# Counting in a threshold search: VectorE masks folded by TensorE in place of counts by VectorE and ScalarE

## The chip, the core and the metric

One NeuronCore of a Trainium2 chip runs the whole kernel. Its engines run side by side and wait for each other through semaphores: TensorE (PE, with its weight loads as PEld), VectorE (DVE), ScalarE (ACT), GpSimd (POOL) and SyncE (SP), which issues DMAs. The metric is device time in microseconds, the median of several executions. The kernel before takes 1645.15 us (three runs, 1643.38 to 1646.12).

## The reference

The reference is a vision tower on 64 images: a patch embedding, one attention block, and a routed feed-forward block. The change lies in the last one, which in short is

```python
acts   = gelu(x @ input_patterns.T).mean(axis=1)          # per image: 2048 numbers
top, i = top_k(acts, 256)                                  # keep the 256 largest of 2048
p      = gelu(scatter(top, i) @ process_input_weights.T)   # per image: 1024 numbers
top, i = top_k(p, 128)
v      = softmax(top) @ process_values[i]                  # per image: 128 numbers
o      = gelu(v @ output_input_weights.T)                  # per image: 2048 numbers
top, i = top_k(o, 256)                                     # keep the 256 largest of 2048
out    = h + (top @ output_patterns[i])                    # the same row for every token
```

The two choices of 256 from 2048 are what is touched.

## The kernel before, in words

`tower` computes everything up to `acts` and stores `h`; `route` does the rest. In `route` the 2048 numbers of an image lie on two partitions of 1024 each (`wide`, 128 partitions x 1024): image b on partitions b and b + 64.

`wide_top_k` finds the 256th largest number of each image exactly. It turns the floats into sortable 32-bit keys and splits each key into two 16-bit words. A search (`look_through`) goes over the high words, a second one over the low words of the numbers that tie there. `wide_top_k` runs twice (`acts` and `o`), so there are four searches. A search has 8 rounds (`ROUNDS`), 32 in all. A round (`try_three`) settles two bits: it asks for three thresholds how many of the image's 2048 words reach each, counts on how many thresholds 256 are reached (`found`), and moves the lower bound by that many steps. `tried` holds the bound and the thresholds of the next round, and `ahead` is the part of the next `tried` that doesn't depend on the answer. The rounds are a strict chain: a round begins when `tried` of the round before is written.

In a round of the kernel before, three engines count:

- VectorE (L1252) compares all 1024 words with the first threshold and 640 of them (`SHARED_AT`) with the second, and adds up by the accumulator of the instruction (`accum_out`).
- ScalarE (`count_too`, L1173 and L1175) takes the Sign of the words against the third threshold, and of the other 384 words against the second; its sums of signs also come from an accumulator.
- TensorE (`sum_halves`, L1068 to L1072) adds the partial counts of the two partitions of an image, and turns signs into counts, by three matmuls of 4 columns with 128x128 matrices (`image_sum`, `image_minus_half`). The result is in one of two PSUM banks (`tallies`).

VectorE then compares three numbers with 256 (`passed`, L1258, with `found` as accumulator) and writes the next `tried` (L1263).

TensorE and ScalarE have other work in the first 16 rounds: `turn_table` transposes the 8 MB of `process_input_weights`, two tables of four 128x128 transposes behind each `sum_halves`, and ScalarE copies each table out of PSUM (`copy_table`, L1181). Each engine takes its instructions in program order, so the transposes of a round sit between two `sum_halves`. SP loads the next 1 MB of the weights when `turned` tells that a buffer is free. In the last 16 rounds neither engine has other work.

Of the kernel before, what the change touches and what calls it, by code (L numbers as in the profile page):

```python
# [20 lines left out]
F32R = mybir.dt.float32r  # L21
I32 = mybir.dt.int32
I16 = mybir.dt.int16
BF16 = mybir.dt.bfloat16
ALU = mybir.AluOpType
ACT = mybir.ActivationFunctionType
AX = mybir.AxisListType

P = 128
# [843 lines left out]
def route(nc, s, w, process_w, process_v, output_w, output_p, search_steps, h2_dram, out):  # L873
# [5 lines left out]
    with ExitStack() as ctx:  # L879
        def sb(name, shape, dt=F32):  # L880
            return ctx.enter_context(nc.sbuf_tensor(name, shape, dt))

        def sem(name):
            return ctx.enter_context(nc.semaphore(name))
# [4 lines left out]
        HALF = s.n_in // 2  # L889
        HALF_T = IN_T // 2  # L890
        ROUNDS = KEY_ROUNDS
        STAGE = 2 * ROUNDS
# [16 lines left out]
        word = sb("word", [P, HALF], I16)  # L909
        low_word = sb("low_word", [P, HALF], I16)  # L910

        reached = [chosen_t[:].bitcast(BF16)[:, n * HALF:(n + 1) * HALF] for n in range(2)]
        SHARED_AT = 5 * HALF // 8
        reached_too = sb("reached_too", [P, 2 * HALF - SHARED_AT], BF16)


        TOKENS = s.tokens // 2
# [27 lines left out]

        tried = sb("tried", [P, 5])
        ahead = sb("ahead", [P, 5])
        blank = sb("blank", [P, 12])
        numbers = sb("numbers", [P, 12], F32R)
        count, signs, offset = (numbers[:, n:n + 4] for n in (0, 4, 8))  # L950
        image_sum = sb("image_sum", [P, P], F32R)
        image_minus_half = sb("image_minus_half", [P, P], F32R)
        passed = sb("passed", [P, 3])
        found = sb("found", [P, 1])
        quota = sb("quota", [P, 1])
# [2 lines left out]

        turn = [ctx.enter_context(nc.psum_tensor(f"rt{b}", [P, 512], F32)) for b in range(3)]
        sums = ctx.enter_context(nc.psum_tensor("sums", [P, 512], F32))  # L960
        tallies = [sums, turn[2]]
        prod = [ctx.enter_context(nc.psum_tensor(f"rp{b}", [P, 512], F32)) for b in range(4)]

        process_in = [sem(f"process_in{n}") for n in range(2)]
        small_in, steps_in, masks_made, turned, copied = sem("small_in"), sem("steps_in"), sem("masks_made"), sem("turned"), sem("copied")
        acts_turned, wide_made, chosen = sem("acts_turned"), sem("wide_made"), sem("chosen")
        words_made, tried_made, numbers_made, counted, counted_too = sem("words_made"), sem("tried_made"), sem("numbers_made"), sem("counted"), sem("counted_too")
        summed, ahead_made, judged = sem("summed"), sem("ahead_made"), sem("judged")
        tie_step, ties_counted, ties_placed = sem("tie_step"), sem("ties_counted"), sem("ties_placed")
        taken, softmax = sem("taken"), sem("softmax")  # L970
# [52 lines left out]
        @block.gpsimd  # L1023
        def _(pool):

            pool.memset(other_half[:], 0.0).then_inc(masks_made, 1)
            pool.wait_ge(masks_made, 1)
            pool.affine_select(out=other_half[:], in_=other_half[:], compare_op=ALU.not_equal, fill=1.0, base=B,
                               pattern=[[-1, P]], channel_multiplier=1).then_inc(masks_made, 1)
            pool.wait_ge(masks_made, 2)  # L1030
            pool.tensor_tensor(same_image[:], other_half[:], w.ident[:], ALU.add).then_inc(masks_made, 1)
            pool.wait_ge(masks_made, 3)
            pool.affine_select(out=same_image[:], in_=same_image[:], compare_op=ALU.not_equal, fill=1.0, base=-B,
                               pattern=[[-1, P]], channel_multiplier=1).then_inc(masks_made, 1)
            pool.memset(blank[:], 0.0).then_inc(masks_made, 1)
            pool.wait_ge(masks_made, 5)
            pool.memset(blank[:, 9:10], (HALF - SHARED_AT) / 2)
            pool.memset(blank[:, 10:11], HALF / 2).then_inc(masks_made, 1)
            pool.memset(values[:, :, s.d_pv:], 1.0).then_inc(masks_made, 1)

        @block.tensor
        def _(pe):

            for t in range(HALF_T):
                last = pe.transpose(turn[t // 4][:, (t % 4) * P:(t % 4 + 1) * P], w.acts[:, t * P:(t + 1) * P],
                                    w.ident[:])
                if t % 4 == 3:
                    last.then_inc(acts_turned, 1)
            pe.wait_ge(masks_made, 7)

            def turn_table(f):
                r, first = tables[f]
# [7 lines left out]

            def sum_halves(n):

                tally = tallies[n % 2][:, 0:4]
                if n == 0:
                    pe.wait_ge(numbers_made, 1)
                if n >= 2:
                    pe.wait_ge(judged, n - 1)
                pe.matmul(tally, image_sum[:], offset, start=True, stop=False)  # L1068
                pe.wait_ge(counted_too, n + 1)
                pe.matmul(tally, image_minus_half[:], signs, start=False, stop=False)  # L1070
                pe.wait_ge(counted, n + 1)
                pe.matmul(tally, image_sum[:], count, start=False, stop=True).then_inc(summed, 1)  # L1072

            def place_ties(stage):

# [84 lines left out]
        def _(act):  # L1160
# [2 lines left out]
                last = act.activation(wide[:, n * 512:(n + 1) * 512], turn[n][:], ACT.Copy, scale=1.0 / s.tokens)  # L1163
            last.then_inc(wide_made, 1)

            def count_too(n, search):


                act.wait_ge(tried_made, n + search + 1)
                if n == 0:  # L1170
                    act.wait_ge(numbers_made, 1)
                with nc.allow_low_precision(reason="whole numbers up to 1024"):
                    act.activation(reached_too[:, 0:HALF], word[:], ACT.Sign, scale=-1.0, bias=tried[:, 4:5],  # L1173
                                   accum_out=signs[:, 2:3])
                    act.activation(reached_too[:, HALF:], word[:, SHARED_AT:], ACT.Sign, scale=-1.0,  # L1175
                                   bias=tried[:, 3:4], accum_out=signs[:, 1:2]).then_inc(counted_too, 1)

            def copy_table(f):
                r, first = tables[f]
                act.wait_ge(turned, f + 1)  # L1180
                act.activation(process_t[:, first:first + 4, r * P:(r + 1) * P],  # L1181
                               prod[f % 4][:].rearrange("p (e j) -> p e j", e=4), ACT.Copy).then_inc(copied, 1)


            act.wait_ge(masks_made, 7)
            act.activation(image_sum[:], same_image[:], ACT.Copy)
            act.activation(image_minus_half[:], same_image[:], ACT.Copy, scale=-0.5)
            act.activation(numbers[:], blank[:], ACT.Copy).then_inc(numbers_made, 1)
            act.activation(both_halves[:], same_image[:, 0:B].unsqueeze(2).to_broadcast([P, B, 2]), ACT.Copy)
            for n in range(STAGE):  # L1190
                count_too(n, n // ROUNDS)
                if n >= 1:
                    copy_table(2 * n - 2)
                    copy_table(2 * n - 1)
            copy_table(fills - 2)
            copy_table(fills - 1)

            def keep_chosen(banks, done):
                for n in range(banks):
# [21 lines left out]
                act.wait_ge(output_product, n + 1)  # L1221
                last = act.activation(wide[:, n * 512:(n + 1) * 512], prod[n][:], ACT.Gelu)
            last.then_inc(wide_made, 1)
            for search in (2, 3):
                for n in range(ROUNDS):
                    count_too(search * ROUNDS + n, search)
            keep_chosen(2, 4)
            act.wait_ge(product, 3)
            act.activation(routed[0][:], prod[2][:, 0:D], ACT.Copy).then_inc(result, 2)
# [2 lines left out]
        def _(dve):  # L1232
# [8 lines left out]
            def look_through(search):  # L1241

                dve.tensor_scalar(tried[:], steps[:, 0:5], float(LOWEST), None, ALU.add).then_inc(tried_made, 1)
                dve.wait_ge(tried_made, search * (ROUNDS + 1) + 1)

                def try_three(search, r):
                    n, at = search * ROUNDS + r, 6 * r
                    if n == 0:
                        dve.wait_ge(numbers_made, 1)
                    with nc.allow_low_precision(reason="whole numbers up to 1024"):  # L1250
                        for m, cols in enumerate((HALF, SHARED_AT)):
                            last = dve.tensor_scalar(reached[m][:, 0:cols], word[:, 0:cols], tried[:, 1 + m:2 + m],  # L1252
                                                     0.0, ALU.is_ge, ALU.add, accum_out=count[:, m:m + 1])
                        last.then_inc(counted, 1)
                    dve.tensor_scalar(ahead[:], steps[:, at + 6:at + 11], tried[:, 0:1], None,
                                      ALU.add).then_inc(ahead_made, 1)
                    dve.wait_ge(summed, n + 1)
                    dve.tensor_scalar(passed[:], tallies[n % 2][:, 0:3], float(s.k_in), 0.0, ALU.is_ge, ALU.add,  # L1258
                                      accum_out=found[:]).then_inc(judged, 1)
                    dve.wait_ge(ahead_made, n + 1)  # L1260
                    dve.wait_ge(judged, n + 1)

                    dve.scalar_tensor_tensor(tried[:], found[:].to_broadcast([P, 5]), steps[:, at + 5:at + 6],  # L1263
                                             ahead[:], ALU.mult, ALU.add).then_inc(tried_made, 1)
                    dve.wait_ge(tried_made, n + search + 2)

                for r in range(ROUNDS):
                    try_three(search, r)
# [113 lines left out]
def search_steps():  # L1382

    size = 4.0 ** np.arange(KEY_ROUNDS - 1, -1, -1)
    rounds = np.stack([0 * size, size, 2 * size, 2 * size - 0.5, 3 * size - 0.5, size], axis=1)
    return np.tile(np.append(rounds.reshape(-1), np.zeros(6)), (P, 1)).astype(np.float32)


# [23 lines left out]
```

## Time and profile before

| | us |
|---|---|
| median of the runs | 1645.15 |
| the profiled execution's own time | 1649.54 |
| its span, from the first instruction to the last | 1647.8 |
| `tower`, to the last copy of `acts` | about 1414 |
| first search, first to last round | 1419.83 to 1444.55 |
| second search | 1447.53 to 1472.22 |
| third search | 1544.55 to 1569.25 |
| fourth search | 1572.23 to 1596.92 |

A timeline row gives the start in us from the span's start, the duration in us, the engine, the line of the code, the operation, what is written and read, the shape and the count; in brackets the idle time of the engine before it and what ended it. The clock column of the stretches (PEclk) is the TensorE clock that was granted, as a share of 2.4 GHz; 0.50 is 1.2 GHz.

### The profile page before, as it was taken

To read this page: it belongs to the slowest core of one execution; us is meant where nothing else is said; L and a number is where in the kernel's file an instruction comes from. 1 tells how busy PE (TensorE), PEld (TensorE's weight loads), DVE (VectorE), ACT (ScalarE), POOL (GpSimd) and SP (SyncE) were. 2 spreads that over 40 slices of the span, in tenths; PEclk is the share of its full clock that TensorE was granted. 3 is DMA by queue.
4 is the path that set the end of the run, shared out by engine and by line. 5 is a ranking of instruction groups with operands and counts; after the bars stand their busy time and mean duration, and the time that the engine had idled before them with its cause. 6 is when DMAs were issued, how large, how long until landed. Compare 5 with 4: busy or idle time off the path is not lost. (4 is left out here: it accounts for less than half of the span.)

```text
span 1647.8 us, 33024 instructions
## 1 busy us (share of the span) xinstructions
PE 1474.3 (89%) x10453; PEld 1420.8 (86%) x10453; DVE 1015.9 (62%) x2493; ACT 882.6 (54%) x3156; POOL 112.4 (7%) x243
## 2 busy tenths in 40 slices
PE   5899999999999999999999999999999998764321
PEld 4799999999999999999999999999999998761220
DVE  6766666656665666665665566566565643585686
ACT  3455555555555555555555555555555554761440
POOL 0000000000000000000000000000000000000000
PEclk9999999999999999999999999999999999757555
DMA  8211111111111111111111111111110000376007
GB/s 202 79 45 45 44 43 43 43 39 40 41 43 43 43 43 43 43 43 43 43 40 40 39 40 39 39 39 40 39 43 10 10 11 11 110 248 249 0 0 313
DMA packets 53094, 99.38 MB, mean 60 GB/s; under 512 B 16704, under 2 KB 35648, under 8 KB 52032
## 3 DMA queue, kind: packets, MB, share of 16 engines
q1 hardware_dynamic: 50768, 96.91, 19.0%
q10 hardware_dynamic: 2288, 2.00, 0.6%
q8 instruction: 19, 0.31, 0.1%
q14 instruction: 19, 0.16, 0.0%
HBM read 73.17 MB, written 25.69 MB: 60 GB/s over the span
## 5 line engine op out<-in xcount | busy, mean ns | idle before, releaser
L620 ACT ACTIVATE ffn<-ffn 128x196 f32<-128x196 f32 x1024 | 329.8, 322 | 220.8 <-PE ffn L511 220.2
L511 PE MATMUL ffn<-x_t_hi,pat_w_hi 128*128 128x392 f32 x1024 | 361.2, 353 | 1.7 <-DVE x_t_lo L783 1.7
L511 PE MATMUL ffn<-x_t_hi,pat_w_lo 128*128 128x392 f32 x1024 | 348.5, 340 | 0.0
L511 PE MATMUL ffn<-x_t_lo,pat_w_hi 128*128 128x392 f32 x1024 | 348.2, 340 | 0.0
L440 PE MATMUL gen<-qkvu_w_hi,h_t_hi 128*98 128x256 f32 x768 | 215.5, 281 | 1.2 <-ACT q_t L578 1.2
L440 PE MATMUL gen<-qkvu_w_hi,h_t_lo 128*98 128x256 f32 x768 | 215.0, 280 | 0.0
L440 PE MATMUL gen<-qkvu_w_lo,h_t_hi 128*98 128x256 f32 x768 | 214.9, 280 | 0.0
L511 PEld LDWEIGHTS ffn<-x_t_hi,pat_w_hi 128*128 128x128 f32 x1024 | 192.8, 188 | 4.1 <-DVE x_t_lo L783 2.0
L620 ACT ACTIVATION_READ_ACCUMULATOR ffn<-ffn 128x1 f32 x1024 | 194.1, 190 | 0.0
L511 PEld LDWEIGHTS ffn<-x_t_lo,pat_w_hi 128*128 128x128 f32 x1024 | 194.0, 189 | 0.0
L511 PEld LDWEIGHTS ffn<-x_t_hi,pat_w_lo 128*128 128x128 f32 x1024 | 192.7, 188 | 0.0
L719 DVE SCALAR_TENSOR_TENSOR shared<-shared,gen 98x512 f32<-98x512 f32 x64 | 44.0, 687 | 167.1 <-ACT shared L593 167.1
L679 DVE TENSOR_TENSOR patch_lo<-pixels,patch_hi 128x392 fp32r<-128x392 f32 x192 | 106.5, 559 | 58.8 <-ACT patch_hi L555 58.6
L394 PE MATMUL gen<-patch_hi,tok_w_hi 128*128 128x392 f32 x384 | 134.2, 350 | 1.6 <-DVE patch_lo L679 1.6
L394 PE MATMUL gen<-patch_hi,tok_w_lo 128*128 128x392 f32 x384 | 131.8, 343 | 0.0
L394 PE MATMUL gen<-patch_lo,tok_w_hi 128*128 128x392 f32 x384 | 131.0, 341 | 0.0
L440 PEld LDWEIGHTS gen<-qkvu_w_hi,h_t_hi 128*98 128x98 f32 x768 | 125.2, 163 | 1.7 <-ACT q_t L578 1.4
L440 PEld LDWEIGHTS gen<-qkvu_w_lo,h_t_hi 128*98 128x98 f32 x768 | 125.3, 163 | 1.5
L440 PEld LDWEIGHTS gen<-qkvu_w_hi,h_t_lo 128*98 128x98 f32 x768 | 125.3, 163 | 0.0
L673 DVE STREAM_TRANSPOSE pixels<-raw 128x448 f32<-128x448 f32 x192 | 111.7, 621 | 12.7 <-DMA raw<-in_x_dram 11.8
L562 ACT ACTIVATE h_t_hi<-gen,bias 128x392 fp32r<-128x392 f32 x64 | 37.6, 588 | 144.2 <-PE gen L394 141.0
L847 POOL TENSOR_SCALAR rstd<-moments 98x4 f32<-98x4 f32 x64 | 22.3, 349 | 1259.5 <-DVE moments L691 1181.0
(209 smaller groups left out, 2735.8 us busy)
## 6 DMA issues: line engine op xcount, KB each, us to landing
raw<-in_x_dram SPq DMA_DIRECT2D x752, 56.0 KB, 2.0
h_dram<-h SPq DMA_DIRECT2D x128, 98.0 KB
process_nat<-ocess_input_weights_dram SPq DMA_DIRECT2D x8, 1024.0 KB, 4.8
process_t<-h_dram SPq DMA_DIRECT2D x8, 896.0 KB, 11.7
out_dram<-process_t SPq DMA_DIRECT2D x8, 896.0 KB, 6.7
h_early<-h_dram SPq DMA_DIRECT2D x4, 896.0 KB, 12.1
out_dram<-h_early SPq DMA_DIRECT2D x4, 896.0 KB, 4.0
pat_nat<-_ffn_input_patterns_dram SPq DMA_DIRECT2D x1, 2048.0 KB, 16.0
```

What stands on the lines that cost most here:

```text
L394: last = pe.matmul(gb[TOK[m]][:, 0:T2], a[:, ks, m * P:(m + 1) * P], b[:, ks], start=n == 0, stop=n == 3 * s.ksubs - 1)
L440: last = pe.matmul(gb[bank][0:T, t * D:(t + 1) * D], a[:, d, tok_cols(img, t)], b[:, d, at:at + D], start=n == 0, stop=n == 3 * s.halves - 1)
L511: last = pe.matmul(fb[f % FFN_BANKS][:, 0:T2], a[:, d, f * P:(f + 1) * P], b[:, d, :], start=n == 0, stop=n == 3 * s.halves - 1)
L562: act.activation(h_ts[0][:, m], gb[TOK[m]][:, 0:T2], ACT.Identity, bias=w.bias[:, m:m + 1])
L620: last = act.activation(cols, cols, ACT.Gelu, accum_out=gelu_sum[:, par, at:at + 1])
L673: last = dve.transpose(pixels[:, 2 * c + h], raw[:, slot, h].rearrange("p i w j -> p w i j"))
L679: dve.tensor_tensor(patch_part(patch[1], ks), turned_pixels(ks), view(patch_part(patch[0], ks)), ALU.subtract).then_inc(patch_low, 1)
L719: dve.scalar_tensor_tensor(flat(gate[:, img]), flat(gate[:, img]), 1.0, gb[(0, 3)[img]][0:T, :], ALU.add, ALU.mult).then_inc(gate_made, 1)
L847: pool.tensor_scalar(rstd[:, which], moments[:, which, :, 1], LN_EPS, None, ALU.add).then_inc(pool_step, 1)
```

## The change

ScalarE no longer counts, and VectorE no longer uses the accumulator. VectorE writes, for each of the three thresholds, a mask of 1024 bf16 ones and zeros per partition (`reached[m]`; the first two lie in `chosen_t` as before, the third in a buffer of its own). For each mask TensorE runs 16 matmuls of 64 columns (`BLOCK`) with the same 128x128 matrix `image_sum`, now bf16, all into the same 64 columns of PSUM: this adds the two partitions of an image and folds 1024 columns into 64. TensorE waits for each mask by itself (`masked`). VectorE then sums the 3 x 64 numbers by a `reduce_sum` from PSUM (`counts`), waits for it, and goes on as before. One PSUM bank (`turn[2]`) takes the place of two. The third threshold is now a whole step, not a half step less as Sign needs it. The small constants for the signs go.

```diff
-        SHARED_AT = 5 * HALF // 8
-        reached_too = sb("reached_too", [P, 2 * HALF - SHARED_AT], BF16)
+        reached.append(sb("reached_last", [P, HALF], BF16)[:])
+        THRESHOLDS, BLOCK = len(reached), 64
...
-        image_sum = sb("image_sum", [P, P], F32R)
-        image_minus_half = sb("image_minus_half", [P, P], F32R)
+        image_sum = sb("image_sum", [P, P], BF16)
+        counts = sb("counts", [P, THRESHOLDS])
...
             def sum_halves(n):
-                tally = tallies[n % 2][:, 0:4]
                 if n == 0:
-                    pe.wait_ge(numbers_made, 1)
-                if n >= 2:
-                    pe.wait_ge(judged, n - 1)
-                pe.matmul(tally, image_sum[:], offset, start=True, stop=False)
-                pe.wait_ge(counted_too, n + 1)
-                pe.matmul(tally, image_minus_half[:], signs, start=False, stop=False)
-                pe.wait_ge(counted, n + 1)
-                pe.matmul(tally, image_sum[:], count, start=False, stop=True).then_inc(summed, 1)
+                    pe.wait_ge(image_sum_made, 1)
+                for m in range(THRESHOLDS):
+                    pe.wait_ge(masked, THRESHOLDS * n + m + 1)
+                    for at in range(0, HALF, BLOCK):
+                        last = pe.matmul(tally[:, m * BLOCK:(m + 1) * BLOCK], image_sum[:],
+                                         reached[m][:, at:at + BLOCK], start=at == 0, stop=at == HALF - BLOCK)
+                last.then_inc(summed, 1)
...
-            for n in range(STAGE):
-                count_too(n, n // ROUNDS)
-                if n >= 1:
-                    copy_table(2 * n - 2)
-                    copy_table(2 * n - 1)
-            copy_table(fills - 2)
-            copy_table(fills - 1)
+            for f in range(fills):
+                copy_table(f)
...
-            for search in (2, 3):
-                for n in range(ROUNDS):
-                    count_too(search * ROUNDS + n, search)
...
                 def try_three(search, r):
                     n, at = search * ROUNDS + r, 6 * r
-                    if n == 0:
-                        dve.wait_ge(numbers_made, 1)
-                    with nc.allow_low_precision(reason="whole numbers up to 1024"):
-                        for m, cols in enumerate((HALF, SHARED_AT)):
-                            last = dve.tensor_scalar(reached[m][:, 0:cols], word[:, 0:cols], tried[:, 1 + m:2 + m],
-                                                     0.0, ALU.is_ge, ALU.add, accum_out=count[:, m:m + 1])
-                        last.then_inc(counted, 1)
+                    for m in range(THRESHOLDS):
+                        dve.tensor_scalar(reached[m], word[:], tried[:, 1 + m:2 + m], None,
+                                          ALU.is_ge).then_inc(masked, 1)
                     dve.tensor_scalar(ahead[:], steps[:, at + 6:at + 11], tried[:, 0:1], None,
                                       ALU.add).then_inc(ahead_made, 1)
                     dve.wait_ge(summed, n + 1)
-                    dve.tensor_scalar(passed[:], tallies[n % 2][:, 0:3], float(s.k_in), 0.0, ALU.is_ge, ALU.add,
+                    dve.reduce_sum(counts[:], tally[:, 0:THRESHOLDS * BLOCK].rearrange("p (m b) -> p m b", b=BLOCK),
+                                   axis=AX.X).then_inc(counted, 1)
+                    dve.wait_ge(counted, n + 1)
+                    dve.tensor_scalar(passed[:], counts[:], float(s.k_in), 0.0, ALU.is_ge, ALU.add,
                                       accum_out=found[:]).then_inc(judged, 1)
...
-    rounds = np.stack([0 * size, size, 2 * size, 2 * size - 0.5, 3 * size - 0.5, size], axis=1)
+    rounds = np.stack([0 * size, size, 2 * size, 3 * size, 3 * size - 0.5, size], axis=1)
```

## Rows read from the trace of the kernel before

**Rows 1.** The page's chain that ended last, shares of the span by line.

```profile
ACT reached_too L1173 2%; PE rp L1097 1%; ACT reached_too L1175 1%; DVE process_t L1352 1%; DVE left L1323 1%; DVE ranked L1322 1%; DVE tried L1263 0%; PE sums L1070 0%; PE rt L1070 0%; DVE h_early L1352 0%; DVE chosen_t L1278 0%; DVE passed L1258 0%; PE rt L1085 0%; PE rp L1148 0%; PE rt L1072 0%
```

**Rows 2.** Timeline of one round of the third search.

```profile
1547.64 1.28 DVE L1252 TENSOR_SCALAR_CACHE_REDUCE chosen_t<-word,tried 128x1024 bf16<-128x1024 int16 x1
...
1548.84 0.88 DVE L1252 TENSOR_SCALAR_CACHE_REDUCE chosen_t<-word,tried 128x640 bf16<-128x640 int16 x1
...
1549.53 0.37 PE L1070 MATMUL rt<-numbers,image_minus_half 128*128 128x4 f32 x1 [2.25 <-ACT reached_too L1175]
1549.64 0.08 DVE L1252 DVE_READ_ACCUMULATOR chosen_t<-word,tried 128x1 fp32r x1
...
1549.78 0.37 PE L1072 MATMUL rt<-numbers,image_sum 128*128 128x4 f32 x1
1549.95 0.33 PEld L1068 LDWEIGHTS sums<-numbers,image_sum 128*128 128x128 f32 x1
...
1550.19 0.16 DVE L1258 TENSOR_SCALAR_CACHE_REDUCE passed<-rt 128x3 f32<-128x3 f32 x1 [0.32 <-PE rt L1072]
...
1550.47 0.23 DVE L1263 SCALAR_TENSOR_TENSOR tried<-found,steps,ahead 128x5 f32<-128x5 f32 x1
...
1550.73 1.28 DVE L1252 TENSOR_SCALAR_CACHE_REDUCE chosen_t<-word,tried 128x1024 bf16<-128x1024 int16 x1
```

**Rows 3.** Stretches (searches 1, 4): length; PE, PEld, DVE, ACT, POOL (count); clock; DMA.

```profile
1419.80:1444.50 24.70, 18.35 (x82) 17.75 (x83) 20.99 (x64) 21.47 (x46) 0.00 (x0) 0.50 0.42 157
...
1572.00:1597.00 25.00, 6.48 (x23) 5.79 (x23) 21.25 (x66) 14.71 (x32) 0.00 (x0) 0.50 0.00 0
```

**Rows 4.** Groups of VectorE by line and shape: busy us, mean ns, idle before.

```profile
L1252 DVE TENSOR_SCALAR_CACHE_REDUCE chosen_t<-word,tried 128x1024 bf16<-128x1024 int16 x32 | 40.9, 1279 | 1.1
...
L1255 DVE TENSOR_SCALAR ahead<-steps,tried 128x5 f32<-128x5 f32 x32 | 7.3, 227 | 0.0
...
L1299 DVE TENSOR_SCALAR sure<-word,tried 128x1024 f32<-128x1024 int16 x2 | 1.5, 754 | 0.1
...
L1334 DVE TENSOR_REDUCE kth<-least 128x1 f32<-128x129 f32 x1 | 0.3, 286 | 0.0
```

**Rows 5.** Groups of PE weight loads: same stationary operand twice, both loaded.

```profile
L497 PEld LDWEIGHTS gen<-wo_w_lo,g_t_hi 128*98 128x98 f32 x256 | 42.8, 167 | 0.0
...
L497 PEld LDWEIGHTS gen<-wo_w_hi,g_t_hi 128*98 128x98 f32 x256 | 42.6, 167 | 13.8 <-DVE g_t_lo L783 13.8
```

**Rows 6.** Timeline: 392-column matmuls at the granted clock 0.50, two in sequence.

```profile
1381.28 0.53 PE L511 MATMUL ffn<-x_t_hi,pat_w_lo 128*128 128x392 f32 x1
1381.60 0.53 PE L511 MATMUL ffn<-x_t_hi,pat_w_hi 128*128 128x392 f32 x1
```

**Rows 7.** Timeline: the same at the full clock, and 32 matmuls of 64 columns.

```profile
1324.91 1.01 PEld L455 LDWEIGHTS gen<-shared 98*64 98x64 f32 x32 [0.26 <-issue]
...
1326.46 0.34 PE L511 MATMUL ffn<-x_t_hi,pat_w_lo 128*128 128x392 f32 x1
...
1326.64 0.34 PE L511 MATMUL ffn<-x_t_hi,pat_w_hi 128*128 128x392 f32 x1
```

**Rows 8.** The same 64-column loads over the whole span, mean ns.

```profile
L455 PEld LDWEIGHTS gen<-shared 98*64 98x64 f32 x1024 | 32.5, 138 | 8.2 <-issue 8.2
```

**Rows 9.** Stretches with PE busy (first figure after the length) and granted clock.

```profile
1426.00:1429.10 3.10, 2.46 (x13) 2.38 (x13) 2.63 (x8) 2.81 (x6) 0.00 (x0) 0.50 0.25 45
1480.00:1482.00 2.00, 2.00 (x10) 1.62 (x11) 0.31 (x1) 0.83 (x2) 0.00 (x0) 0.50 1.01 419
...
1486.00:1488.00 2.00, 2.00 (x13) 0.56 (x9) 0.00 (x0) 0.00 (x0) 0.00 (x0) 1.00 1.01 419
1531.60:1535.40 3.80, 3.67 (x16) 3.30 (x16) 0.03 (x1) 0.00 (x0) 0.00 (x0) 0.50 0.00 0
...
40.00:42.00 2.00, 0.82 (x7) 0.58 (x6) 2.00 (x6) 2.00 (x6) 0.00 (x0) 1.00 0.41 118
```

**Rows 10.** Timeline of a round of the first search: the transposes behind the count.

```profile
1428.40 1.97 PE L1057 MATMUL rp<-ident,process_nat 128*128 128x128 f32 x8
```

More of the change, by code:

```diff
@@ L947, in route @@
         ahead = sb("ahead", [P, 5])
-        blank = sb("blank", [P, 12])
-        numbers = sb("numbers", [P, 12], F32R)
-        count, signs, offset = (numbers[:, n:n + 4] for n in (0, 4, 8))
-        image_sum = sb("image_sum", [P, P], F32R)
-        image_minus_half = sb("image_minus_half", [P, P], F32R)
+        image_sum = sb("image_sum", [P, P], BF16)
+        counts = sb("counts", [P, THRESHOLDS])
         passed = sb("passed", [P, 3])
@@ L960, in route @@
         sums = ctx.enter_context(nc.psum_tensor("sums", [P, 512], F32))
-        tallies = [sums, turn[2]]
+        tally = turn[2]
         prod = [ctx.enter_context(nc.psum_tensor(f"rp{b}", [P, 512], F32)) for b in range(4)]
@@ L966, in route @@
         acts_turned, wide_made, chosen = sem("acts_turned"), sem("wide_made"), sem("chosen")
-        words_made, tried_made, numbers_made, counted, counted_too = sem("words_made"), sem("tried_made"), sem("numbers_made"), sem("counted"), sem("counted_too")
+        words_made, tried_made, image_sum_made, counted, masked = sem("words_made"), sem("tried_made"), sem("image_sum_made"), sem("counted"), sem("masked")
         summed, ahead_made, judged = sem("summed"), sem("ahead_made"), sem("judged")
@@ L1034, in _ @@
                                pattern=[[-1, P]], channel_multiplier=1).then_inc(masks_made, 1)
[L1035 to L1038, printed above, removed]
             pool.memset(values[:, :, s.d_pv:], 1.0).then_inc(masks_made, 1)
@@ L1048, in _ @@
                     last.then_inc(acts_turned, 1)
-            pe.wait_ge(masks_made, 7)
+            pe.wait_ge(masks_made, 5)
             def turn_table(f):
@@ L1164, in _ @@
             last.then_inc(wide_made, 1)
-            def count_too(n, search):
-                act.wait_ge(tried_made, n + search + 1)
-                if n == 0:
-                    act.wait_ge(numbers_made, 1)
-                with nc.allow_low_precision(reason="whole numbers up to 1024"):
[L1173 to L1176, printed above, removed]
             def copy_table(f):
@@ L1182, in copy_table @@
                                prod[f % 4][:].rearrange("p (e j) -> p e j", e=4), ACT.Copy).then_inc(copied, 1)
[L1185 to L1188, printed above, removed]
+            act.wait_ge(masks_made, 5)
+            act.activation(image_sum[:], same_image[:], ACT.Copy).then_inc(image_sum_made, 1)
             act.activation(both_halves[:], same_image[:, 0:B].unsqueeze(2).to_broadcast([P, B, 2]), ACT.Copy)
-            for n in range(STAGE):
-                count_too(n, n // ROUNDS)
-                if n >= 1:
-                    copy_table(2 * n - 2)
-                    copy_table(2 * n - 1)
-            copy_table(fills - 2)
-            copy_table(fills - 1)
+            for f in range(fills):
+                copy_table(f)
             def keep_chosen(banks, done):
@@ L1247, in try_three @@
                     n, at = search * ROUNDS + r, 6 * r
-                    if n == 0:
-                        dve.wait_ge(numbers_made, 1)
-                    with nc.allow_low_precision(reason="whole numbers up to 1024"):
-                        for m, cols in enumerate((HALF, SHARED_AT)):
-                            last = dve.tensor_scalar(reached[m][:, 0:cols], word[:, 0:cols], tried[:, 1 + m:2 + m],
-                                                     0.0, ALU.is_ge, ALU.add, accum_out=count[:, m:m + 1])
-                        last.then_inc(counted, 1)
+                    for m in range(THRESHOLDS):
+                        dve.tensor_scalar(reached[m], word[:], tried[:, 1 + m:2 + m], None,
+                                          ALU.is_ge).then_inc(masked, 1)
                     dve.tensor_scalar(ahead[:], steps[:, at + 6:at + 11], tried[:, 0:1], None,
```

## The prediction

> **What bounds the kernel now.** I read the chain that ended last first: behind `tower`, whose work the change leaves alone, its largest share by line is ScalarE's counting at L1173 and L1175, together 3% of the span [rows 1]. So the rounds lie on the path to the end; there are 32, and nothing else hides them. Next the timeline of one round [rows 2]. From the first count (1547.64) to the first count of the next round (1550.73) are 3.09 us, in five steps: VectorE's two counts until the second accumulator is read (1549.64 + 0.08 = 1549.72), 2.08; to the last small matmul (1549.78), 0.06; from its start to `passed` on VectorE (1550.19), 0.41; to the writing of `tried` (1550.47), 0.28; to the next round (1550.73), 0.26. ScalarE is no worse than level with VectorE: the matmul that waits for it starts at 1549.53, and the one behind it only 0.06 after VectorE's count. Hence taking ScalarE out gains nothing by itself; only a shorter path over VectorE and TensorE can. The stretches of the searches [rows 3] show the same period with transposes beside it (24.7 us for 8 rounds) and without (25.0). In both the granted TensorE clock is 0.50, that is 1.2 GHz. 32 x 3.09 = 98.9 us is all that the change acts on.
>
> **The change part by part.**
>
> *Masks.* Three compares of 1024 words take the place of a count of 1024 and one of 640 columns. A count of 1024 takes 1279 ns [rows 4]. Without the accumulator the nearest row is L1299: the same int16 words, a scalar from `tried`, but 4-byte output, 754 ns. The mask writes 2 bytes per number. Its fixed part is at least the 227 ns of L1255, the same operation on 5 numbers. No row shows 2 bytes in and 2 bytes out, so the mask lies between 0.23 and 0.75 us, at worst 1.28; I take the middle of the first two, 0.49, since half the bytes of L1299's result go out. An instruction starts about 0.08 us before its predecessor's recorded end (1.28 long, followed after 1.20 [rows 2]), so masks come every 0.40. By the Trainium skill, "VectorE: DVE Perf Modes", "The perf-mode tier table", a scalar operation on 16-bit data in SBUF runs at four numbers a cycle against two for fp32; 754 ns less half of L1299's 533 ns of streaming at 0.96 GHz would be an estimated 0.49, the same.
>
> *TensorE.* Three matmuls of 4 columns go; 48 of 64 columns come, and 48 weight loads with them, for each matmul of this program loads its own weights: L497 meets the same g_t_hi twice in a row, under wo_w_hi and wo_w_lo, and both have 256 loads [rows 5]. So the term is the pitch of a pair, load and matmul. At the granted clock 0.50, 392-column pairs follow every 0.32 to 0.33 us [rows 6], 0.83 ns a column, with the load of 128 columns wholly hidden; for 64 columns that gives 0.053, the lower end there. At the full clock the pitch is 0.18 [rows 7], 15 ns above 392 columns at 2.4 GHz (163 ns); 64 columns would give 27 to 41 ns. L455 is nearest in size: 32 loads of 64 columns, in 1.01 us, the last one 138 ns long [rows 7, 8]: (1.01 - 0.14) / 31 = 28 ns at the full clock, so 56 at half. The upper end is the small pair of fp32r here: L1072 starts at 1549.78, the next load at 1549.95, 0.17 [rows 2]; half of that, 0.085, if it goes by the bytes of the load. I take 0.056, by L455. Mask two comes 0.40 after mask one, while its 16 predecessors need 0.90: TensorE is behind from the first mask on, and only the first mask and 47 pitches lie on the path.
>
> *The fold's end.* From the last pair to VectorE I take the 0.41 of the small matmul plus 60 more columns at 1.2 GHz, 0.05: 0.46. `reduce_sum` over 192 numbers is new and wholly on the path: L1334 takes 286 ns for 129 numbers [rows 4], 63 more at the 1.04 ns by which the counts of 1024 and 640 columns differ (1.28 and 0.88 us [rows 2]) are 0.07; with 0.03 for its wait, 0.38. A reduction that read PSUM for nothing extra is the cheap end; 0.15 more is the dear one. `passed` and `tried` stay, 0.28 and 0.26. `ahead` is hidden under the pairs.
>
> *Sum at half clock.* 0.49 + 0.05 + 47 x 0.056 (2.63) + 0.46 + 0.38 + 0.28 + 0.26 = 4.55 us a round, against 3.09: 1.46 more. 32 times is 46.7 us. On the profiled execution's 1649.54 (span 1647.8, and 1.7 around it) that gives 1696.2; this execution is 4.4 above the median of the runs, so 1645.15 + 46.7 = 1692.
>
> *What is hidden or nothing.* In the first 16 rounds eight transposes stand between the last pair and the next first pair [rows 10]. They take 1.97 to the end of the last; the gap they sit in is 0.46 + 0.38 + 0.28 + 0.26 + 0.49 + 0.05 = 1.92, and the last one's drain doesn't hold up the next load. Where this cover is short it costs 0.05 to 0.2 a round, at most 3 us in all. Table copies on ScalarE come earlier, for nobody: the tables' consumer runs after the second search. The weight loads that SP issues on `turned` keep their two rounds of lead, in longer rounds. The single PSUM bank adds no wait, for the next masks follow the reduction anyway. The small memsets and copies at the start (the wait for 5 in place of 7) end before the first mask.
>
> **The rivals.**
>
> *A. TensorE reaches 2.4 GHz in the rounds.* In a round of the first search PE was busy 2.46 of 3.10 us and the clock stayed 0.50; dense work from 1480 on had the full clock by 1486; 3.67 busy of 3.80 at 1531.6 had not; and at 40 us, 0.82 busy of 2.00 kept the full clock once there [rows 9]. In the first 16 rounds pairs and transposes would fill nearly the whole round (2.63 + 1.97 of 4.55), which speaks for a rise; in the last 16 PE idles 1.9 us a round, which speaks against. At the full clock, with the 41 ns of the 392-column rows: 0.49 + 0.05 + 1.93 + 0.43 + 0.38 + 0.54 = 3.82, 0.73 more. All 32: 1668; the first 16 only: 1645.15 + 11.7 + 23.4 = 1680.
>
> *B. The load is not hidden behind 64 columns.* All rows that hide a load have longer matmuls or fewer weight columns. At 0.085 a pair: 0.54 + 4.00 + 0.46 + 0.92 = 5.92, 2.83 more, 90.5 in all: 1736. The dear mask of 0.75 adds 8: 1744. The Trainium skill, "TensorE: Matmul & The Clock Gate", "Back-to-back issue gap", speaks for this: load-and-matmul streams of 128 columns hold at about 81 ns each, 28 above the columns' own time; an estimate by it is 54 ns a pair at the full clock and 81 at half, 1730 where all is at half. The trace agrees only in part: 15 ns of excess at the full clock, none at half.
>
> *C. The masks bound, not TensorE: faster.* From 25 ns a pair downward at the full clock 16 pairs fit into the 0.40 between masks, and the round is 0.49 + 0.80 + 0.05 + 15 x 0.025 + an end of 0.26 (in place of 0.46, if the drain shrinks with the clock) + 0.38 + 0.54 = 2.90: 0.19 less, 6 us, 1639. With the end at 0.41 it is 3.05, 1644, no change. For it speaks that L455 comes near 28 ns; against it that those have half the weight columns, and that the clock was 0.50 in every search.
>
> *D. The masks run like the counts.* With 1.28 the masks follow every 1.20: 1.28 + 2.40 + 0.05 + 15 x 0.056 + 0.46 + 0.92 = 5.95, 1737. L1299 without an accumulator speaks against it.
>
> **How the numbers follow.** Forecast (half clock, hidden loads) 0.45, with a range of its own of 1684 to 1708; A 0.25; B 0.16; C 0.10; D 0.04. The likeliest gives 1692. For 8 in 10 I leave out C and part of A below 1657 and the dear end of B and D above 1740. About 0.2% (3.3 us) is what a measurement of this kernel can tell from no change: C splits into 0.06 faster and 0.04 the same, all else is slower, 0.90.
>
> **What would show it.** Pitch of the 48 pairs: 0.056 (forecast), near 0.04 with a granted clock of 1.00 (A), 0.08 or more (B). The masks' duration: 0.49, with the second mask's pairs never waiting; if PE waits for VectorE before each mask it is C or D. `reduce_sum` 0.35. Period of a round 4.55 in all four searches, and `tower` unchanged. I am wrong if the period is below 3.0, or if the clock rises in the first search alone and the two pairs of searches differ by 0.7 a round.

## The result, and the profile after

| | us |
|---|---|
| before, median of 5 runs | 1645.29 (1643.38 to 1648.89) |
| after, median of 5 runs | 1653.15 (1652.14 to 1657.29) |
| ratio, 95% interval | 1.0044 (1.0029 to 1.006) |
| profiled execution: its own time, its span, before | 1649.54, 1647.8 |
| profiled execution: its own time, its span, after | 1652.14, 1650.4 |

The change makes the kernel slower: by the ratio it is 0.44%, and the medians lie 7.9 us apart, where 46.7 were forecast. The chain of waits of the kernel after gives the rounds to TensorE: the fold's matmuls (L1061), the masks (L1218) and the reduction (L1223) stand where ScalarE's counts stood in [rows 1].

```profile
PE rt L1061 3%; PE rp L1088 1%; DVE process_t L1320 1%; DVE chosen_t L1218 1%; DVE left L1291 1%; DVE counts L1223 1%; DVE ranked L1290 1%; DVE tried L1231 0%; DVE h_early L1320 0%; DVE chosen_t L1246 0%; DVE passed L1226 0%; PE rt L1076 0%; PE rp L1139 0%; DVE process_nat L1320 0%; DVE sure L1242 0%
```

What the chain doesn't say is that there are two kinds of round. In the fourth search it shows them one above the other (start, duration, what): 48 pairs end the wait after 2.76 us three times, and after 1.59 us from then on.

```profile
1571.97 2.76 PE rt L1061 x48
...
1576.21 2.76 PE rt L1061 x48
...
1580.46 2.76 PE rt L1061 x48
...
1584.71 1.59 PE rt L1061 x48
...
1587.79 1.59 PE rt L1061 x48
```

The stretches say why (length, busy time of the engines with counts, then the granted clock). The first rounds of a search run at 0.50, 1.2 GHz, or end in the rise; the rest has the full clock, where the kernel before had 0.50 in the whole search [rows 3].

```profile
1418.40:1422.70 4.30, 3.69 (x54) 3.72 (x55) 2.15 (x8) 0.02 (x1) 0.00 (x0) 0.50 0.38 160
1422.70:1443.30 20.60, 17.00 (x389) 15.43 (x388) 14.42 (x52) 7.68 (x14) 0.00 (x0) 0.99 0.44 155
...
1542.60:1546.90 4.30, 2.74 (x48) 2.58 (x48) 2.19 (x10) 0.00 (x0) 0.00 (x0) 0.60 0.00 0
1546.90:1567.40 20.50, 10.94 (x336) 10.19 (x336) 14.41 (x52) 0.00 (x0) 0.00 (x0) 1.00 0.01 2
1571.40:1584.20 12.80, 8.23 (x144) 7.76 (x144) 6.54 (x25) 0.00 (x0) 0.00 (x0) 0.52 0.01 1
1584.20:1599.60 15.40, 7.87 (x240) 7.28 (x240) 10.84 (x41) 0.00 (x0) 0.00 (x0) 1.00 0.01 2
```

A round at 0.50 takes 4.25 us (the very first 4.33); in this execution there are six, one at the head of each of the first three searches and three in the fourth. The 26 others take 3.08, within 0.01 of the round before [rows 2]. So the rounds lose 6 x (4.25 - 3.09) = 7.0, less 26 x 0.01. One timeline for each kind; first a round at 0.50:

```profile
1542.64 0.88 DVE L1218 TENSOR_SCALAR chosen_t<-word,tried 128x1024 bf16<-128x1024 int16 x2
...
1543.19 1.89 PE L1061 MATMUL rt<-chosen_t,image_sum 128*128 128x64 bf16 x32 [4.74 <-DVE chosen_t L1218]
1543.44 0.48 DVE L1218 TENSOR_SCALAR reached_last<-word,tried 128x1024 bf16<-128x1024 int16 x1
...
1544.88 1.04 PE L1061 MATMUL rt<-reached_last,image_sum 128*128 128x64 bf16 x16
1545.96 0.36 DVE L1223 TENSOR_REDUCE counts<-rt 128x3 f32<-128x192 f32 x1 [1.90 <-PE rt L1061]
1546.36 0.16 DVE L1226 TENSOR_SCALAR_CACHE_REDUCE passed<-counts 128x3 f32<-128x3 f32 x1
...
1546.63 0.23 DVE L1231 SCALAR_TENSOR_TENSOR tried<-found,steps,ahead 128x5 f32<-128x5 f32 x1
```

and one at the full clock:

```profile
1562.28 0.88 DVE L1218 TENSOR_SCALAR chosen_t<-word,tried 128x1024 bf16<-128x1024 int16 x2
...
1562.83 1.11 PE L1061 MATMUL rt<-chosen_t,image_sum 128*128 128x64 bf16 x32 [1.50 <-DVE chosen_t L1218]
...
1563.77 0.63 PE L1061 MATMUL rt<-reached_last,image_sum 128*128 128x64 bf16 x16
1564.44 0.36 DVE L1223 TENSOR_REDUCE counts<-rt 128x3 f32<-128x192 f32 x1 [0.74 <-PE rt L1061]
1564.83 0.16 DVE L1226 TENSOR_SCALAR_CACHE_REDUCE passed<-counts 128x3 f32<-128x3 f32 x1
...
1565.36 0.49 DVE L1218 TENSOR_SCALAR chosen_t<-word,tried 128x1024 bf16<-128x1024 int16 x1
```

The first 32 pairs give the pitch: (1544.88 - 1543.19) / 32 = 52.8 ns at 0.50, (1563.77 - 1562.83) / 32 = 29.4 at the full clock. The first is 64 columns at 1.2 GHz (53.3), the second 2.7 ns above 64 columns at 2.4 GHz: the weight load is hidden at both. The pairs of the third mask follow without a gap, so TensorE, not VectorE, bounds the fold. From the last pair (47 pitches behind the first) to the reduction are 0.29 and 0.23, and from the reduction to the next round 0.93 and 0.92. The masks take 481 to 484 ns:

```profile
L1218 DVE TENSOR_SCALAR chosen_t<-word,tried 128x1024 bf16<-128x1024 int16 x32 | 14.1, 484 | 0.6
L1218 DVE TENSOR_SCALAR reached_last<-word,tried 128x1024 bf16<-128x1024 int16 x16 | 7.7, 481 | 0.0
L1223 DVE TENSOR_REDUCE counts<-rt 128x3 f32<-128x192 f32 x16 | 5.7, 358 | 16.5 <-PE rt L1061 16.5
```

The two profiled executions differ by 2.6 only, for two things outside of the rounds ran the other way. The first round began 1.45 earlier; the chain is that much earlier already at the transposes of `acts` that open `route`, ahead of what the change touches. And between the second and the third search, 2.77 were saved, with a granted clock of 0.73 in the mean there, against 0.64 before. Below, after and then before; the line of after begins 1 us before the end of its last round, at 1473.08:

```profile
1472.10:1542.50 70.40, 29.32 (x136) 15.14 (x134) 40.63 (x82) 10.95 (x19) 0.00 (x0) 0.73 0.52 204
```

```profile
1472.22:1544.55 72.33, 33.03 (x134) 16.43 (x133) 40.00 (x78) 11.06 (x19) 0.00 (x0) 0.64 0.51 200
```

That saving isn't the change's own: of the kernels below, which differ little there, two have it and five have not (their way from the second search to the third is 69.4 and 69.5, or 71.7 to 72.5, against 72.33 before and 69.56 after). Rounds +6.9, between the searches -2.8, the start -1.45: +2.6. The medians differ by 7.9, about the rounds' share. The five executions of the changed kernel also part by their mean granted clock: 0.962 to 0.963 in the three from 1652.14 to 1653.15, 0.960 and 0.959 in the two at 1656.72 and 1657.29.

### The profile page after: what moved, and what is told of

Same layout as the page of the kernel before. It is cut to its first block and busy times, and to the rows that moved or that the text cites. A ratio compares the mean times of both kernels' runs of the same rounds, so it can differ in the third digit from the quotient of the medians.

```text
span 1650.4 us, 35769 instructions
## 1 busy us (share of the span) xinstructions
PE 1489.9 (90%) x11893; PEld 1436.4 (87%) x11893; DVE 1001.2 (61%) x2493; ACT 824.1 (50%) x3026; POOL 112.0 (7%) x240
```

## The experiments

In the expectations, "theory C" is the reading that the loss is the rounds at 0.50; it is not the prediction's rival C. "Filling" is matmuls whose result nobody reads.

**Filling before each search.** Is the whole loss the six rounds at 0.50? Ten fp32 matmuls of `ident` with itself, into columns that nobody reads, go to TensorE ahead of the first mask of each search; the pairs still wait for that mask.

```diff
+            def warm(calls, into):
+                for _ in range(calls):
+                    pe.matmul(into[:, 256:384], w.ident[:], w.ident[:], start=True, stop=True)
...
             def sum_halves(n):
+                if n % ROUNDS == 0:
+                    warm(10, sums)
```

> The changed kernel with ten idle-time fp32 matmuls (128 columns, ident by ident, into unused columns of the bank `sums`) in front of the first count of each search, so that TensorE does not come to it from rest. Theory C (the loss is the rounds at the granted clock 0.50, some 4.25 us each against 3.08 at the full clock; six such rounds in the trace of the changed kernel): all 32 rounds at 3.08, about 7 us less than the changed kernel, 1646 us, level with the kernel before. Rival F (the fold's path is longer at any clock, the half-clock rounds are a side show): 1652 to 1655, as the changed kernel. Rival W (the filling matmuls come late and hold up the first masks): above 1655.

Measured: 1647.91 against 1646.88 for the kernel before, ratio 1.0000 (0.9991 to 1.001). Every round but the very first (3.17) takes 3.07 to 3.09, and the clock is 1.00 in all four searches; two of them:

```profile
1416.00:1443.00 27.00, 20.98 (x461) 19.17 (x460) 19.54 (x68) 7.86 (x15) 0.00 (x0) 1.00 0.47 182
...
1568.00:1594.00 26.00, 13.30 (x384) 12.28 (x383) 19.32 (x64) 0.00 (x0) 0.00 (x0) 1.00 0.01 2
```

The loss of 0.44% is gone with the rounds at 0.50. What remains is a round as long as before.

**The kernel before, kept busy.** Is the full clock what the change gave, and would the kernel before have used it as well? The same filling goes into the kernel before: 10 matmuls before each search, 3 or 8 behind each `sum_halves`.

```diff
             def sum_halves(n):
...
+                if n % ROUNDS == 0:
+                    warm(10, turn[0] if n else prod[0])
...
+                warm(3 if n < STAGE else 8, turn[0])
```

> The kernel before, with fp32 filling matmuls in TensorE's idle time: ten in front of each search, three behind each count in the first two searches, eight in the last two. Theory C: the small matmuls of the counts, too, pay for the granted clock 0.50; with the clock up, the step from the last small matmul to VectorE falls from 0.41 to about 0.26 us and the round from 3.09 to 2.94: 32 times 0.15 is 5 us, 1640. Rival F (before, VectorE's and ScalarE's counts of 2.08 us set the round, TensorE's clock is of no weight): 1645, or more where the filling comes late.

Measured: 1643.91, ratio 0.9983 (0.9973 to 0.9993), with rounds of 2.98 to 2.99 but for two: the second of the first search takes 3.62, at a clock of 0.50 with PE busy throughout (3.60 of 3.60 us), and the second of the third search 3.09. The direction is right, the gain smaller than expected (0.10 a round): the step from the last small matmul to VectorE is 0.31 here, 0.41 in [rows 2].

```profile
1556.77 0.27 PE L1078 MATMUL rt<-numbers,image_sum 128*128 128x4 f32 x1
...
1557.08 0.16 DVE L1265 TENSOR_SCALAR_CACHE_REDUCE passed<-rt 128x3 f32<-128x3 f32 x1 [0.22 <-PE rt L1078]
```

So at the full clock the counts of before are 0.09 a round shorter than masks and fold (2.99 against 3.08), and at 0.50 they are 1.16 shorter.

**Blocks of 32 columns.** Is the pitch of a pair set by its columns or by something else? 96 pairs of 32 columns take the place of 48 of 64.

```diff
-        THRESHOLDS, BLOCK = len(reached), 64
+        THRESHOLDS, BLOCK = len(reached), 32
```

> The changed kernel with 32 columns a block in place of 64: 96 pairs of load and matmul a round in place of 48, the same columns. Theory C with a pair that costs its columns (load hidden): pitch about 16 ns at the full clock, round 3.1. Rival L (a pair has a floor near the 29 ns seen for 64 columns, because of the load or the issue): 96 x 0.028 = 2.7 us of pairs, round 4.3, about 38 us more than the changed kernel, near 1690.

Measured: one execution, 1683.52, rounds of 3.96 at the full clock and 4.15 at 0.50. Three rounds of the first two searches take 4.8 to 5.0: in each PE stands still for 0.7 to 0.8 us between two pairs, waiting for nothing that the profile shows. A round at the full clock, in the first search:

```profile
1428.41 1.76 PE L1061 MATMUL rt<-chosen_t,image_sum 128*128 128x32 bf16 x64 [0.49 <-DVE chosen_t L1218]
1430.02 0.95 PE L1061 MATMUL rt<-reached_last,image_sum 128*128 128x32 bf16 x32
```

and one at 0.50, in the fourth:

```profile
1587.14 1.89 PE L1061 MATMUL rt<-chosen_t,image_sum 128*128 128x32 bf16 x64 [1.40 <-DVE chosen_t L1218]
...
1588.87 1.01 PE L1061 MATMUL rt<-reached_last,image_sum 128*128 128x32 bf16 x32
```

1.61 / 64 = 25.2 ns and 1.73 / 64 = 27.0. At 0.50 the columns (26.7) still set the pitch; at the full clock, where they would need 13.3, something else sets it, near 25 ns, and the clock gives nearly nothing. The rival with a floor was right in kind, with 25 in place of 29 ns; whether the load or the issue makes it, no run separates. Of the widths tried, 64 gives the shortest round (3.08, against 3.96 with 32 and 3.22 with 128, below).

**Half of the fold.** Only the first 512 columns of each mask are folded, 24 pairs: the other half of the numbers is not counted, so the thresholds found are not the reference's. Does the clock follow how much TensorE has to do?

```diff
-                    for at in range(0, HALF, BLOCK):
+                    for at in range(0, HALF // 2, BLOCK):
...
-                                         reached[m][:, at:at + BLOCK], start=at == 0, stop=at == HALF - BLOCK)
+                                         reached[m][:, at:at + BLOCK], start=at == 0, stop=at == HALF // 2 - BLOCK)
```

> The changed kernel, folding only the first 512 of the 1024 columns of each mask (24 pairs a round in place of 48); the counts, and so the numbers chosen, are not the reference's. Theory C with the clock following how busy TensorE is: in the last two searches the clock stays 0.50, round 0.54 + 23 x 0.053 + 0.28 + 0.40 + 0.53 = 2.97. Rival F (the clock has nothing to do with it, or stays up): masks bound, round about 2.7, at the clock 1.00. By either the time falls below the changed kernel: 1649 against 1639.

Measured: one execution, 1641.14, between the two times expected, for half of the rounds went each way. The first two searches, with transposes beside the fold, rise; the last two, without, stay at 0.50 throughout:

```profile
1418.00:1440.00 22.00, 17.51 (x253) 14.70 (x253) 17.14 (x63) 7.71 (x14) 0.00 (x0) 0.87 0.51 183
...
1540.00:1562.00 22.00, 10.23 (x168) 9.13 (x168) 16.34 (x59) 0.00 (x0) 0.00 (x0) 0.50 0.00 1
```

The round is 2.70 at the full clock and 2.97 at 0.50. Both follow from the terms above. At the full clock eight pairs (0.24) fit between two masks, and the masks bound: 0.54 + 0.80 + 7 x 0.0294 + 0.23 + 0.92 = 2.70. That is rival C's mechanism, which half the pairs bring about and 48 do not. At 0.50 the pairs bound: 0.54 + 23 x 0.0528 + 0.29 + 0.92 = 2.96.

**Two masks on TensorE, the third threshold on ScalarE.** If pairs at the full clock bound the round, fewer of them should beat both kernels, and ScalarE is free to count. It takes the third threshold by Sign, as before the change; the counts enter through one small matmul into the third block, whose last column holds the constant that turns signs into counts. The filling stands before each search and behind each fold.

```diff
-                for m in range(THRESHOLDS):
-                    pe.wait_ge(masked, THRESHOLDS * n + m + 1)
+                for m in range(MASKS):
+                    pe.wait_ge(masked, MASKS * n + m + 1)
...
-                last.then_inc(summed, 1)
+                pe.wait_ge(counted_too, n + 1)
+                pe.matmul(tally[:, MASKS * BLOCK:MASKS * BLOCK + 4], image_minus_half[:], signs[:],
+                          start=True, stop=True).then_inc(summed, 1)
+                warm(1 if n < STAGE else 4, turn[0])
...
+            def count_too(n, search):
+                act.wait_ge(tried_made, n + search + 1)
+                with nc.allow_low_precision(reason="whole numbers up to 1024"):
+                    act.activation(signs_of[:], word[:], ACT.Sign, scale=-1.0, bias=tried[:, 4:5],
+                                   accum_out=signs[:, 2:3]).then_inc(counted_too, 1)
```

> VectorE masks only the first two thresholds and TensorE folds only these (32 pairs); ScalarE counts the third by Sign and its accumulator, as in the kernel before; one small fp32r matmul of 4 columns adds its sums, and the reduction over 3 x 64 numbers stays. Ten filling matmuls stand before the first fold of a search, one or four behind each fold. If TensorE's fold at the full clock is what keeps the round of the changed kernel at 3.08 us, dropping 16 pairs takes 16 x 0.029 = 0.47 off, and the small matmul puts some 0.1 back: 2.70 to 2.75 us a round at a granted clock of 1.00, 11 to 12 us less than the kernel before in 32 rounds: 1633 to 1637. Rival: ScalarE's count (1.39 to 1.48 us after the round begins) and the small fp32r matmul behind it set the end, and its path costs as much as the 16 pairs: 3.0 to 3.1 a round, 1643 to 1647.

Measured: 1637.48 (1636.34 to 1638.06) against 1646.49, ratio 0.9941 (0.9928 to 0.9955): 0.6% faster than the kernel before, and below every time of the changed kernel. All rounds but the second of the first search take 2.70; that one takes 3.08, as VectorE stands still for 0.49 before it writes `tried`, and the trace doesn't say for what:

```profile
1553.10 1.15 ACT L1180 ACTIVATE signs_of<-word,tried 128x1024 bf16<-128x1024 int16 x1 [1.46 <-DVE tried L1269]
1553.10 0.88 DVE L1256 TENSOR_SCALAR chosen_t<-word,tried 128x1024 bf16<-128x1024 int16 x2
...
1553.64 1.11 PE L1078 MATMUL rt<-chosen_t,image_sum 128*128 128x64 bf16 x32 [0.51 <-DVE chosen_t L1256]
...
1554.15 0.19 ACT L1180 ACTIVATION_READ_ACCUMULATOR signs_of<-word,tried 128x1 fp32r x1
...
1554.58 0.25 PE L1081 MATMUL rt<-signs,image_minus_half 128*128 128x4 f32 x1
1554.67 0.97 PEld L1065 LDWEIGHTS rt<-ident 128*128 128x128 f32 x8
1554.70 1.02 PE L1065 MATMUL rt<-ident 128*128 128x128 f32 x7
1554.87 0.36 DVE L1261 TENSOR_REDUCE counts<-rt 128x3 f32<-128x192 f32 x1 [0.75 <-PE rt L1081]
```

ScalarE is ready at 1554.34; the small matmul starts at 1554.58, right behind the 32 pairs (1553.64 + 32 x 0.0294). The pairs still bound, and the rival with ScalarE at the end is refuted. The median missed the expected range by 0.5: in the profiled execution the first round began at 1420.77, 2.3 later than with the first filling (1418.47), a difference that is there already at the transposes of `acts` (1415.38 against 1413.09).

**The same without filling.** The last edit with its calls of `warm` taken out.

```diff
-                if n % ROUNDS == 0:
-                    warm(10, sums)
...
-                warm(1 if n < STAGE else 4, turn[0])
```

> As the run before, without any filling matmul. If the clock follows how busy TensorE is, the first two searches (transposes beside the pairs) rise to the full clock after a few rounds, at about 2.7 us a round, and the last two stay at 0.50: 0.54 + 31 x 0.0528 + 0.1 + 0.3 to 0.4 + 0.39 + 0.27 + 0.26 = 3.5 us a round. 16 x 3.5 + 16 x 2.75 = 100 us, 1 more than the kernel before: about 1647, and 11 to 13 us more than the run with the filling. Rival: 32 pairs a round are enough for the full clock as 48 are: all but the first rounds of a search at 2.7, within 4 us of the run with the filling.

Measured: one execution, 1652.84. The rounds are as expected by the first theory: 2.70 in the first two searches behind a slow start of two rounds each (3.51 to 3.61), 3.55 to 3.57 in the last two. The rows are the third search with filling and without:

```profile
1540.00:1560.00 20.00, 16.30 (x320) 15.00 (x320) 13.03 (x52) 9.53 (x16) 0.00 (x0) 1.00 0.01 3
```

```profile
1538.00:1560.00 22.00, 11.22 (x183) 10.81 (x184) 12.48 (x42) 7.45 (x12) 0.00 (x0) 0.54 0.00 1
...
1564.00:1585.00 21.00, 10.49 (x174) 10.08 (x172) 11.69 (x39) 6.21 (x10) 0.00 (x0) 0.50 0.01 2
```

16 x 0.86 = 13.8 of the 14.8 us between the two profiled executions come from the last two searches; the slow starts of the first two add 3.1, and the first round began 2.0 earlier. Taking 16 pairs off the path without keeping TensorE busy loses what it was to gain. The total was expected at 1647, with 100 us for the 32 rounds. In the trace they take 103.4, for the four slow rounds of the first two searches and for 3.56 where 3.5 was expected; where the rest of the 6 us lies, a single execution doesn't say.

**Blocks of 128 columns.** With the first filling, so that the clock is out of the question.

```diff
-        THRESHOLDS, BLOCK = len(reached), 64
+        THRESHOLDS, BLOCK = len(reached), 128
```

> The changed kernel with ten filling matmuls before each search, and blocks of 128 columns in place of 64: 24 pairs in place of 48, and a reduction over 384 numbers in place of 192. If the pitch at the full clock is set by the columns (64 in 29.4 ns, 1.1 ns over their 26.7 at 2.4 GHz, or 53.3 for 128), 24 pairs at 0.055 take 1.31 in place of 1.41, and the reduction 192 x 1.04 ns = 0.20 more: 3.15 to 3.2 us a round, 2 to 4 us above the run with blocks of 64 and filling: 1650 to 1652. Rival, the gap of back-to-back pairs: 81 ns for a pair of 128 columns: 1.94 for the fold, 3.8 us a round, 1671.

Measured: one execution, 1648.86, rounds of 3.21 to 3.23 at a clock of 1.00.

```profile
1562.21 1.07 PE L1067 MATMUL rt<-chosen_t,image_sum 128*128 128x128 bf16 x16 [1.70 <-DVE chosen_t L1224]
1563.12 0.61 PE L1067 MATMUL rt<-reached_last,image_sum 128*128 128x128 bf16 x8
1563.76 0.56 DVE L1229 TENSOR_REDUCE counts<-rt 128x3 f32<-128x384 f32 x1 [0.68 <-PE rt L1067]
```

0.91 / 16 = 56.9 ns a pair, 3.6 above the columns (with 64 columns it is 2.7, not the 1.1 of the expectation); the reduction over 384 numbers takes 0.56, 0.20 more, as expected. The time itself is 1 to 3 us better than expected; the way from the second search to the third was the short one here (69.5).

By the Trainium skill, "TensorE: Matmul & The Clock Gate", "Back-to-back issue gap", load-and-matmul pairs of 128 columns hold at about 81 ns; the 56.9 measured doesn't bear it out. The Trainium skill, same page, "Wait — 56ns, not 53.3ns?", gives the columns at 2.4 GHz and 2.5 ns more, and never below about 25 ns: by it an estimated 55.8, 29.2 and 25 for 128, 64 and 32 columns, against 56.9, 29.4 and 25.2 here, where each matmul has its load.

## Why the prediction was wrong

**The step that failed is the clock.** "Sum at half clock" stood for all 32 rounds; 26 had the full clock. At the measured terms this is 26 x 1.17 = 30.4 us, most of the 39 by which the forecast was too high. The argument was that the clock was 0.50 in every search of before [rows 3], and that PE idles 1.9 us a round in the last 16. But the change itself replaces what TensorE does in a round: three matmuls of 4 columns become 48 of 64. In the third search a PE busy 10.94 of 20.50 us kept the full clock; in the half fold, a PE busy 10.23 of 22.00 never got it. The row that should have weighed more stood among those quoted: 0.82 busy of 2.00 at the full clock [rows 9].

**The other steps, at half clock.** The masks were right (0.49 forecast, 0.48 measured, one every 0.40), in part by luck: by the rows 0.49 was the middle of 0.23 and 0.75, and that no row shows 2 bytes in and 2 bytes out was not so. The copies that split the keys (L1296, L1297) go from int16 to int16, reading every second word, and take 693 and 684 ns for 1024 numbers; by them the masks would have come out 0.2 too dear. The reduction was right too (0.38 against 0.40 with its wait), and so was the way from `passed` to the next round. The pitch was 0.0528, not 0.056: the lower end given, columns and nothing else. The fold's end was mis-sized: 0.46 forecast, 0.29 measured. The 0.41 came from a lone 4-byte matmul of 4 columns; whether the type, the width or the pairs running ahead make the fold's end shorter, no run separates. Together 0.15 + 0.17, less 0.02, is 0.30 a round: 4.55 forecast, 4.25 measured, 9.6 us over all rounds. So 46.7 - 30.4 - 9.6 = 6.7, against 6.9 measured in the rounds.

**Rival A had the clock and the wrong price.** It said 3.82 a round at the full clock; 3.08 was measured. 47 x (0.041 - 0.0294) = 0.55 is the pitch, 0.43 - 0.23 = 0.20 the fold's end. This was inconsistent: for the forecast I took 28 ns from L455 [rows 7] and doubled it, and for A I took 41 from the 392-column rows. With 28 ns and the 0.26 that rival C had for the end, A would have been 0.54 + 1.32 + 0.26 + 0.92 = 3.04, 1643.5: no change, 0.04 a round off what 26 rounds did. The range ended at 1657 because of this price. Besides, all rounds or the first 16 were the only two cases for the clock; the true one, a slow start in each search, was not thought of.

**The others.** B falls: 29.4 and 52.8 ns, loads hidden. D falls with the masks' 0.48. C's mechanism is real, but needs fewer pairs (the half fold) or a pitch of 25 ns or less, where 64 columns take 29.4. The transposes cost nothing, as said: 3.08 in searches with and without them. Of the two signs named as proof against the forecast neither came (the period was not below 3.0, and the clock rose in all searches); the period of 3.08 instead of 4.55 alone refutes it.

**What stays open.** Why the fourth search of the changed kernel needs three rounds to rise and the third one, and what decides how early the clock rises between the second and the third search. The spread of its executions goes with the mean granted clock, but only one of them left a trace: whether the others had more slow rounds or lost the saving between the searches isn't known.

## What to carry to other kernels

Here the granted clock went with the work in a stretch, not with its place in the kernel: where a change gives TensorE more work or takes it away, price both levels with the same row, and look for a slow start of each burst as well as for all or nothing. A chain that alternates between VectorE and short bursts of TensorE can be kept at the full clock by filling matmuls where TensorE waits anyway; here that was worth 0.44% for the changed kernel, 0.17% for the kernel before, and it decided whether sharing the counts won or lost (1637.48 with it, 1652.84 in the one execution without). And where one engine bounds a round and another has been freed, give back the part that fits beside it: 1637.48 came from two thresholds on one way and one on the other.

## What the runs showed of the hardware

A pair of load and matmul with 128 weight columns in bf16 runs at the pitch of its own columns at 0.50 (27.0 ns for 32 columns, 52.8 for 64), and at the full clock 2.7 to 3.6 ns above it (29.4 for 64, 56.9 for 128), but 25.2 for 32 columns, which by themselves would need 13.3.

The recorded busy time doesn't tell whether the clock rises. With blocks of 32 columns PE was busy 2.74 of 4.00 us in the fourth search and mostly stayed at 0.50, with one short rise that didn't hold:

```profile
1578.00:1582.00 4.00, 2.58 (x96) 2.47 (x96) 2.09 (x9) 0.00 (x0) 0.00 (x0) 0.93 0.01 2
1586.00:1590.00 4.00, 2.74 (x96) 2.64 (x96) 1.92 (x9) 0.00 (x0) 0.00 (x0) 0.50 0.02 4
```

With blocks of 64, PE was no busier (2.74 of 4.30 at 1542.60), and the full clock came and stayed.
